# Decoder kernel on one core: second attention taken batch by batch between the expert rows' gathers, and another order in the first attention's slot part

## The chip, the cores and the metric

One core of a Trainium2 chip. The time is device time of one execution, in microseconds (us), median of the runs. Engines: PE is TensorE (matmuls and transposes), DVE VectorE, ACT ScalarE, POOL GpSimd, SP SyncE (which issues most DMAs). Each engine takes its own list of instructions in order, and waits on semaphores that the others raise.

## The reference

Two decoder layers on x of 4 batches, 256 tokens, 256 features (1024 tokens in all), each sublayer followed by residual and layer norm:

```python
x = _layernorm(x + _L0_attn_ref(x, ...))            # slot attention, 16 heads, running sums over tokens
x = _layernorm(x + _L0_xattn_ref(ctx_1024, x, ...)) # state-space scan
x = _layernorm(x + _L0_ffn_ref(x, ...))             # 64 experts, 6 per token, and a shared one
x = _layernorm(x + _L1_attn_ref(x, ...))            # linear attention, 16 heads: the second attention
x = _layernorm(x + _L1_xattn_ref(x, ctx_1024, ...)) # cross attention, 32 heads, rotary positions
x = _layernorm(x + _L1_ffn_ref(x, ...))             # ternary weights
```

The second attention, with heads of 16 features, is

```python
Q = jax.nn.elu(Q) + 1.0
K = jax.nn.elu(K) + 1.0
KV = jnp.einsum('bhsd,bhse->bhde', K, V)
QKV = jnp.einsum('bhsd,bhde->bhse', Q, KV)
out = QKV / (QK_sum[..., None] + 1e-08)
```

followed by the output projection. K and V are summed within one batch, so batches are independent of each other up to and through this sublayer and the projections behind it.

## The kernel before

All work is written out by hand, one list per engine; nothing is planned by a program. Tokens lie in 8 tiles of 128 (`TILES`), two tiles per batch. `xres` holds the residual by token, `xT` its transpose, and `ps` is PSUM with 8 banks.

First attention: a loop over 8 pairs of heads (`step`). In it PE projects values and gates of each tile (`project_vg(t)`, L629, two banks in turn, so tile t waits for the gate of tile t-2, counted from tile 2). ACT copies the values and takes the tanh of the gate (`values_and_gate`), DVE multiplies (`gate(t)`, L1634). Between tiles run the slots: transposes of `okT` (L652), maximum and shift on DVE (L1649, L1651), the exponent `slot_exp` on ACT, its sum and a small product on DVE (L1655, L1659), slot transposes on PE (L661), `wT` on DVE (L1666), then `read(b)` on PE (L594), the mask on DVE (L1621) and `mix(b)` (L681). `read(1)` uses the bank of the gates and waits for gate 7. ACT's order is tiles 0 to 3, slot exponent, tiles 4 and 5, a decay, tiles 6 and 7. PE does tiles 4 to 7 and then the slot transposes. At the same time POOL and DVE run the scan of the second sublayer, whose products POOL makes (L1149, L1156, L1159).

Experts: PE runs groups of four blocks of 128 rows, DVE writes each output (L1931), SP stores it to `y_dram`. When the last is stored, POOL gathers for each token tile its 6 rows, 48 indirect DMAs into a ring of 8 buffers `yg` (L1231). DVE adds each, weighted (L1968); gather n waits for the addition of n-8. After a tile's sixth row DVE takes its statistics (L1615, L1616).

Only when all 48 are added follow, for all four batches at once: layer norm (`norm(2)`, L1776; ACT makes the scale), transposes (`turn_x`, L774) and their copies to `xT` on ACT, query projection (L910), keys and values (L917), the elu in parts on DVE and ACT (L1983 to L2008), key-value products (L928, L930), mask (L2014), read (L941), division (L2018 to L2021), transposes (L951), output projection (L962), residual and statistics (L2030), norm (`norm(3)`), transposes, query projection of the cross attention (L977), rotation (`rotate`, L1901, L1906), the split of the rotated queries into three bf16 parts (casts on ACT, rests on DVE, L2049) and their copies into the stack `q_st` (L1921). The head transposes of the cross attention (L990) then wait for everything stacked, and for POOL's memsets of `q_st`, which wait for `norm(3)` to be complete (L1236). SP's loads of the last layer's weights wait for the same.

## Time and profile before

| | |
|---|---|
| runs | 1192.13, 1201.07, 1199.13 us; median 1199.13 |
| profiled execution | 1193.41 us, its span (first to last instruction) 1191.6 us |
| busy in the span | PE 940.7 us (79%), DVE 809.4 (68%), ACT 499.5 (42%), POOL 374.2 (31%) |
| mean granted clock of TensorE | 0.888 of full |
| chain that ended last | PE 43%, DVE 27%, waiting for nothing shown 8%, DMA 6%, ACT 6%, POOL 6% |

A row of the timeline or of the groups reads: line, engine, operation, output<-inputs, shapes, count, and in brackets the idle time of that engine before it with what ended it. A busy share says how full an engine is and not whether it is late; for that one reads which wait ended last at a place. PE at half clock shows as a granted clock of 0.50 (1.2 GHz against 2.4).

### The profile page before, as it was taken

What the parts mean: (1) busy time and instruction counts of PE and PEld (TensorE: products, weight loads), DVE (VectorE), ACT (ScalarE), POOL (GpSimd) and SP (SyncE); (2) the same over time, 40 slices, a digit from 0 to 9 for tenths busy, and PEclk for the clock granted to TensorE, in tenths of its full rate; (3) what the DMA queues carried; (4) which work ended last, traced back from release to release, by engine and by line L of the source; (5) the groups of instructions that cost most, each with busy time, mean ns of one, the idle gap of its engine ahead of it and who ended that gap; (6) DMA issues with size and microseconds to landing.
All of it is one profiled execution on the core that took longest, in us unless ns stands there. A gap on an engine that the chain in (4) does not pass through costs nothing.

```text
span 1191.6 us, 17024 instructions
## 1 busy us (share of the span) xinstructions
PE 940.7 (79%) x5419; PEld 602.9 (51%) x5423; DVE 809.4 (68%) x1458; ACT 499.5 (42%) x852; POOL 374.2 (31%) x270
## 2 busy tenths in 40 slices
PE   6699998989999899588999899600975776888575
PEld 2366565655656565456666667400573433444333
DVE  6568787777868686968355566344878995555766
ACT  3535344444453444433433345300224444767164
POOL 0035554637273745610433233276010000000000
PEclk9799999999999999779999899855997766989787
DMA  4801121111111111071699999633010000000001
GB/s 156 270 19 66 58 79 53 57 53 57 66 62 49 61 44 45 1 194 38 189 295 297 276 279 290 141 106 97 1 55 17 1 0 1 1 0 1 1 1 36
DMA packets 52585, 104.60 MB, mean 88 GB/s; under 512 B 7513, under 2 KB 25057, under 8 KB 52033
## 3 DMA queue, kind: packets, MB, share of 16 engines
q1 hardware_dynamic: 46785, 88.37, 23.2%
q0 software_dynamic: 5760, 15.74, 5.3%
q8 instruction: 20, 0.33, 0.1%
q14 instruction: 20, 0.16, 0.0%
HBM read 87.14 MB, written 16.94 MB: 87 GB/s over the span
## 4 chain that ended last, share of the span: by engine, by line
PE 43%; DVE 27%; issue 8%; DMA 6%; ACT 6%; POOL 6%; SPq 2%; DVEq 0%; ACTq 0%; POOLq 0%
PE ps L629 6%; PE ps L713 4%; POOL yg L1231 3%; PE ps L594 3%; PE ps L584 3%; PE ps L804 3%; PE ps L990 3%; DVE row_max L2057 3%; PE ps L816 3%; DMA w_dn<-in_w_dn 3%; DMA y_dram<-y_out 2%; PE ps L642 2%; DVE state L1610 2%; PE ps L1033 2%; DVE on L1683 1%
## 5 line engine op out<-in xcount | busy, mean ns | idle before, releaser
L1156 POOL TENSOR_TENSOR state<-state,c_row 128x1024 f32<-128x1024 f32 x32 | 77.3, 2417 | 200.6 <-DVE state L1610 118.0
L629 PE MATMUL ps<-w_vg,xT 128*128 128x512 f32 x256 | 117.8, 604 | 10.2 <-DVE th L1634 10.2
L1204 POOL DMA_INDIRECT xg<-x_dram,tok_of x68 | 65.3, 961 | 154.1 <-PE ps L862 103.9
L1149 POOL TENSOR_TENSOR drive<-du,b_row 128x1024 f32<-128x1024 f32 x32 | 89.4, 2796 | 56.2 <-DVE y L1760 56.2
L804 PE MATMUL ps<-w_gv,xgT 128*128 128x352 f32 (+1 forms) x272 | 91.4, 481 | 1.3 <-DVE y_out L1931 1.3
L1621 DVE TENSOR_TENSOR aT<-ps,tri 128x768 f32<-128x768 f32 x64 | 59.2, 954 | 42.1 <-PE ps L594 42.1
L584 PE MATMUL ps<-xT,w_qks 128*128 128x512 f32 x192 | 85.0, 593 | 0.7 <-DMA w_qks<-in_wqks 0.7
L1610 DVE TENSOR_TENSOR_SCAN state<-decay,drive 128x1024 f32<-128x1024 f32 x32 | 83.5, 2612 | 0.0
L629 PEld LDWEIGHTS ps<-w_vg,xT 128*128 128x128 f32 x256 | 46.6, 192 | 64.7 <-issue 45.5
L2057 DVE TENSOR_REDUCE row_max<-ps 128x1024 f32 x64 | 74.1, 1216 | 7.2 <-PE ps L1005 6.3
L1159 POOL TENSOR_TENSOR y<-y,state 128x1024 f32<-128x1024 f32 x32 | 75.3, 2354 | 2.5
L774 PE MATMUL ps<-ident,xres 128*128 128x128 f32 x64 | 12.9, 365 | 78.3 <-DVE xres L1776 78.3
L1634 DVE SCALAR_TENSOR_TENSOR th<-th,ps 128x256 f32<-128x256 f32 x64 | 26.7, 418 | 66.2 <-ACT th L1260 65.1
L816 PE MATMUL ps<-w_dn,hidT 88*128 88x256 f32 (+1 forms) x272 | 71.2, 384 | 0.0
L1249 POOL COPY v_cols<-x_v 128x64 f32 x32 | 8.6, 270 | 197.7 <-PE ps L1033 181.9
L1931 DVE TENSOR_SCALAR y_out<-ps 128x256 f32<-128x256 f32 x68 | 28.9, 424 | 58.9 <-PE ps L816 31.8
L1260 ACT ACTIVATE probT<-ps 128x1024 f32<-128x1024 f32 x64 | 61.7, 1026 | 14.8 <-PE ps L1019 14.8
L804 PEld LDWEIGHTS ps<-w_gv,xgT 128*128 128x128 f32 x272 | 50.6, 196 | 26.3 <-issue 4.6
L713 PE MATMUL ps<-w_o,oT 128*128 128x256 f32 x256 | 61.8, 391 | 0.0
L1260 ACT ACTIVATE qsT<-ps 128x1024 bf16<-128x1024 bf16 x32 | 32.8, 1024 | 61.8 <-PE ps L990 61.8
L584 PEld LDWEIGHTS ps<-xT,w_qks 128*128 128x128 f32 x192 | 35.4, 190 | 40.2 <-issue 38.5
L1231 POOL DMA_INDIRECT yg<-y_dram,slot_idx x48 | 45.4, 945 | 27.5 <-issue 14.0
(291 smaller groups left out, 2103.9 us busy)
## 6 DMA issues: line engine op xcount, KB each, us to landing
w_gv<-in_w_gv SPq DMA_DIRECT2D x68, 352.0 KB
w_dn<-in_w_dn SPq DMA_DIRECT2D x68, 176.0 KB
y_dram<-y_out SPq DMA_DIRECT2D x68, 128.0 KB, 6.8
b_row<-x_dbl_dram SPq DMA_DIRECT2D x16, 512.0 KB, 3.6
c_row<-x_dbl_dram SPq DMA_DIRECT2D x16, 512.0 KB, 4.7
y_dram<-blank SPq DMA_DIRECT2D x4, 1408.0 KB, 13.0
w_vg<-in_wvg SPq DMA_DIRECT2D x8, 512.0 KB, 3.3
w_qks<-in_wqks SPq DMA_DIRECT2D x8, 384.0 KB, 3.0
```

Source lines behind the costliest of these rows:

```text
L584: last = mm(bank(PJ + n % 2), w_qks[:, k, part * P:(part + 1) * P], xT[:, k, half * 512:(half + 1) * 512], start=(k == 0), stop=(k == KD - 1))
L629: last = mm(bank(PJ + t % 2), xT[:, k, t * P:(t + 1) * P], w_vg[:, k, :], start=(k == 0), stop=(k == KD - 1))
L713: last = mm(ps[:, X + b % 2, 256 * t:256 * t + 256], oT[:, h, c:c + P], w_o[:, h, :], start=(h == 0), stop=(h == 1))
L804: last = mm(ps[:, j, 0:2 * F], x_of(k), w(k), start=(k == 0), stop=(k == KD - 1))
L816: last = mm(ps[:, bk, 256:512], hidT[:, j, f * P:(f + 1) * P], w(f), start=(f == 0), stop=(f == 1))
L1149: G.tensor_tensor(drive[:, n % 2], du[:, e], b_row[:, j], ALU.mult).then_inc(drive_ready, 1)
L1156: G.tensor_tensor(state[:, n % 2], state[:, n % 2], c_row[:, j], ALU.mult).then_inc(read_out, 1)
L1159: G.tensor_tensor(y[:, e], y[:, e], state[:, n % 2], ALU.add).then_inc(y_added, 1)
L1231: G.indirect_dma_start(yg[:, n % 8, :], None, y_dram, bass.IndirectOffsetOnAxis(ap=slot_idx[:, n // TOPK, n % TOPK:n % TOPK + 1], axis=0)) ...
L1260: return nc.scalar.activation(out, in_, func, **kw)
L1610: V.tensor_tensor_scan(state[:, n % 2], decay[:, n % 2], drive[:, n % 2], 0.0, ALU.mult, ALU.add).then_inc(scanned, 1)
L2057: V.tensor_reduce(row_max[:, bass.ds(i * 16 + 4 * b, 4)], pair(4 + 2 * (b % 2)).rearrange("p (a k) -> p a k", a=4), AX.X, ALU.max).then_in ...
```

## The change

Second attention. Each batch is begun when its two tiles are fully added. Five rounds are written out: round r starts batch r (norm, transposes, projections, elu, key-value product, read) and ends batch r-1 (division, output projection, residual, norm, cross attention's query projection, rotation, split and stack). Batches use banks 0 to 3 and 4 to 7 in turn. DVE's list has the additions of gathered rows (`combine`) put between these steps, 12 per round in rounds 0 to 2, after 12 ahead of round 0. Elementwise work takes the two tiles of a batch in one instruction; the buffers `lqT`, `lk`, `lv`, `l_out` shrink to two batches. ACT splits the queries into positive and negative part (four Relu per batch), which DVE did, and makes three of the six stack copies. Keys and queries share `rot`, `part` and `rotated_f32`, and `q_st` and `yg` move in memory (`gap` keeps a stretch free). POOL's and SP's lists are unchanged; their waits for `normed` 32 now mean that the last batch's second norm is done.

First attention. ACT takes tile 4 ahead of the slot exponent, PE does the slot transposes ahead of tile 7, and DVE's `wT` comes ahead of gate 7.

The diff, cut to its core (all it takes away in the second attention is left out; so are `project_out_l`, `attend_l`, `project_x`, `divide_l` and the like, which do for one batch what the old lines did for all):

```diff
+    for r in range(B + 1):
+        for kind, late in kinds:
+            if 0 <= r - late < B:
+                turns[kind, r - late] = len(turns) + 1
+    return turns
...
+NORMED = in_turn(("x2", 0), ("x3", 1))
+SUMMED = {("x2", 0): 1, ("x2", 1): 2, ("x3", 0): 3, ("x2", 2): 4, ("x3", 1): 5, ("x2", 3): 6, ("x3", 2): 7, ("x3", 3): 8}
+MASKED = in_turn(("out", 1), ("kv", 0))
...
+        lqT = sb("lqT", [P, 2, KD, 256])
+        lq_low = sb("lq_low", [P, 2, KD, 256])
+        lk = sb("lk", [P, 2, 2, D])
+        lk_low = sb("lk_low", [P, 2, 2, D])
+        lv = sb("lv", [P, 2, 2, D])
...
+        l_out = sb("l_out", [P, 2, 2, D])
...
-                for t in range(4, TILES):
+                for t in range(4, TILES - 1):
                     project_vg(t)
...
+                project_vg(TILES - 1)
...
+                        c = (2 * b + t) * P
+                        last = mm(ps[:, bank_n, t * 256:(t + 1) * 256], xT[:, k, c:c + P], w[:, k, :], start=(k == 0),
+                                  stop=(k == KD - 1))
+                last.then_inc(done, 1)
+
+            def project_l(b, base):
+                pe.wait_ge(normed, 16 + 2 * NORMED["x2", b])
+                if b >= 2:
+                    pe.wait_ge(attended, b - 1)
+                turn_pair(xres[:, 2 * b:2 * b + 2, :], base)
+                pe.wait_ge(xT_copied, 4 + TURNED["x2", b])
+                for m in range(KD):
+                    for k in range(KD):
+                        last = mm(ps[:, base + 1, m * 256:(m + 1) * 256], l_wq[:, k, m * P:(m + 1) * P],
+                                  xT[:, k, b * 256:(b + 1) * 256], start=(k == 0), stop=(k == KD - 1))
+                last.then_inc(lproj_ready, 1)
+                if b >= 2:
+                    pe.wait_ge(turns_done, 4 * (TILES + b - 1))
+                for t in range(2):
+                    c = (2 * b + t) * P
+                    for k in range(KD):
...
+            for r in range(B + 1):
+                new, old = 4 * (r % 2), 4 * ((r + 1) % 2)
+                if r < B:
+                    project_l(r, new)
+                if r:
+                    project_out_l(r - 1, old)
+                if r < B:
+                    attend_l(r, new)
+                if r:
+                    project_x(r - 1, old)
...
-                for t in range(2, 4):
+                for t in range(2, 5):
                     values_and_gate(t)
                 act.wait_ge(slots_shifted, at(i, 1, 1))
                 f(slot_exp[:], okn[:], ACT.Exp, scale=DK ** -0.5).then_inc(slots_exp, 1)
-                for t in range(4, 6):
-                    values_and_gate(t)
+                values_and_gate(5)
                 decay_of(i, 1)
...
+            def elu_q(b, base):
+                act.wait_ge(lproj_ready, 2 * b + 1)
+                for m in range(KD):
+                    src = ps[:, base + 1, m * 256:(m + 1) * 256]
+                    f(lqT[:, b % 2, m], src, ACT.Relu, bias=l_bq[:, m:m + 1])
+                    last = f(lq_low[:, b % 2, m], src, ACT.Relu, bias=l_nbq[:, m:m + 1], scale=-1.0)
+                last.then_inc(act_step, 1)
+                act.wait_ge(act_step, PAIRS + 2 + b + 1)
+                f(lq_low[:, b % 2], lq_low[:, b % 2], ACT.Exp, scale=-1.0).then_inc(elu_exp, 1)
+
+            def elu_k(b):
+                act.wait_ge(elu_split, b + 1)
+                f(lk_low[:, b % 2], lk_low[:, b % 2], ACT.Exp).then_inc(elu_exp, 1)
...
+            for r in range(B + 1):
+                new, old = 4 * (r % 2), 4 * ((r + 1) % 2)
+                if r < B:
+                    scale_pair("x2", r)
+                    copy_pair("x2", r, new)
+                    elu_q(r, new)
+                if r:
+                    copy_pair("att", r - 1, old + 1)
+                if r < B:
+                    elu_k(r)
+                if r:
+                    scale_pair("x3", r - 1)
+                    copy_pair("x3", r - 1, old + 1)
+                    split_q(r - 1)
...
-                for t in range(6, TILES):
-                    gate(t)
+                gate(6)
                 for n in range(2):
                     c = slice(n * 512, (n + 1) * 512)
                     dve.wait_ge(w_turned, at(i, 2, n + 1))
                     V.tensor_tensor(wT[:, c], bank(Y + n), zT[:, c], ALU.mult).then_inc(wT_copied, 1)
+                gate(7)
...
+            combine_next = iter(range(TILES * TOPK))
+
+            def combine(count):
+
+                for n in itertools.islice(combine_next, count):
+                    t, k = n // TOPK, n % TOPK
                     dve.wait_ge(back[n % 8], 16 * (n // 8 + 1))
                     dve.wait_ge(combined, B + n)
                     V.scalar_tensor_tensor(out=xres[:, t, :], in0=yg[:, n % 8, :], scalar=pick_w[:, t, k:k + 1],
                                            in1=xres[:, t, :], op0=ALU.mult, op1=ALU.add).then_inc(combined, 1)
-                dve.wait_ge(combined, B + TOPK * (t + 1))
-                stats_of(t)
-            norm(2)
-
+                    if k == TOPK - 1:
+                        dve.wait_ge(combined, B + n + 1)
+                        stats_of(t, 2)
...
+            def take_kv(b, base):
+                both = ps[:, base + 2:base + 4, :]
+                dve.wait_ge(lproj_ready, 2 * b + 2)
+                then(V.tensor_tensor(lk[:, b % 2], both[:, :, 0:D], l_bkv[:, 0:D].unsqueeze(1).to_broadcast([P, 2, D]),
+                                     ALU.add))
+                V.tensor_scalar(lk_low[:, b % 2], lk[:, b % 2], 0.0, None, ALU.min).then_inc(elu_split, 1)
+                V.tensor_tensor(lv[:, b % 2], both[:, :, D:2 * D], l_bkv[:, D:2 * D].unsqueeze(1).to_broadcast([P, 2, D]),
+                                ALU.add)
+
...
+            combine(2 * TOPK)
...
+            for r in range(B + 1):
+                new, old = 4 * (r % 2), 4 * ((r + 1) % 2)
+                if r < B:
+                    norm_pair("x2", r)
+                    combine(1)
+                if r:
+                    divide_l(r - 1, old)
+                    combine(1)
+                if r < B:
+                    take_kv(r, new)
+                    combine(2)
+                if r:
+                    add_out_l(r - 1, old)
+                    combine(1)
+                if r < B:
+                    add_bias("x2", r, l_bo)
+                    finish_elu(r)
+                    combine(2)
+                    mask_kv(r, new)
+                    combine(1)
+                if r:
+                    norm_pair("x3", r - 1)
+                    combine(1)
+                    rotate_q(r - 1, old)
+                    combine(1)
+                    add_bias("x3", r - 1, x_bo)
+                    rest_q(r - 1, 0)
+                    combine(1)
+                    rest_q(r - 1, 1)
+                    combine(1)
+                    stack_q(r - 1)
+                else:
+                    combine(6)
```

## Rows read from the trace of the kernel before

**Rows 1.** The page's 40 slices: PE's busy tenths and its granted clock.

```profile
PE   6699998989999899588999899600975776888575
...
PEclk9799999999999999779999899855997766989787
```

**Rows 2.** Windows: busy us (instructions) of PE, PEld, DVE, ACT, POOL; clock, DMA, GB/s.

```profile
770.80:832.90 62.10, 0.00 (x0) 0.00 (x0) 27.52 (x63) 0.00 (x0) 45.38 (x48) 0.50 0.35 102
...
832.90:909.80 76.90, 55.58 (x256) 40.33 (x256) 63.30 (x178) 21.56 (x35) 5.66 (x6) 0.88 0.07 28
```

**Rows 3.** Instructions on the gathered rows: duration ns min/median/max, first and last start.

```profile
L1231 POOL DMA_INDIRECT yg<-y_dram,slot_idx x48: 942/946/955, 770.8 to 829.6; - x48
L1968 DVE SCALAR_TENSOR_TENSOR xres<-yg,pick_w,xres x48: 483/484/486, 773.6 to 832.4; 128x256 f32<-128x256 f32 x48
```

**Rows 4.** Timeline of the first attention, fourth pair, and a start in the fifth.

```profile
237.55 1.06 ACT L1260 ACTIVATE slot_exp<-okn 128x1024 f32<-128x1024 f32 x1 [2.88 <-DVE okn L1651]
...
239.18 0.42 DVE L1634 SCALAR_TENSOR_TENSOR th<-th,ps 128x256 f32<-128x256 f32 x1 [1.67 <-ACT th L1260]
...
239.66 3.70 PE L629 MATMUL ps<-w_vg,xT 128*128 128x512 f32 x8 [1.26 <-DVE th L1634]
...
240.98 0.97 DVE L1659 SCALAR_TENSOR_TENSOR eps_sq<-slot_sum 128x16 f32<-128x16 f32 x1
...
243.20 1.04 PE L661 MATMUL ps<-ident,slot_exp 128*128 128x128 f32 x8
...
245.16 1.58 PE L594 MATMUL ps<-wT,eT 64*128 64x256 f32 x16 [0.93 <-DVE wT L1666]
246.14 0.96 DVE L1621 TENSOR_TENSOR aT<-ps,tri 128x768 f32<-128x768 f32 x1 [0.43 <-PE ps L594]
...
298.71 1.04 PE L661 MATMUL ps<-ident,slot_exp 128*128 128x128 f32 x8
```

**Rows 5.** Groups by shape between 770.8 and 909.8: count, busy us, mean ns.

```profile
L1983 DVE TENSOR_TENSOR lqT<-lqT,lq_low 128x512 f32<-128x512 f32 x4 | 2.7, 685 | 0.1
...
L917 PE MATMUL ps<-l_wkv,xT 128*128 128x512 f32 x32 | 13.9, 592 | 0.0
...
L928 PE MATMUL ps<-lv,lk 128*128 128x128 f32 x32 | 5.4, 293 | 0.0
...
L930 PE MATMUL ps<-ones,lk 128*128 128x8 f32 x32 | 4.1, 236 | 0.0
```

**Rows 6.** Timeline from the last gather to the head transposes.

```profile
834.33 2.67 DVE L1776 TENSOR_SCALAR xres<-xres,ln_rstd,ln_shift 128x256 f32<-128x256 f32 x8
...
835.21 3.40 PE L774 MATMUL ps<-ident,xres 128*128 128x128 f32 x16 [67.51 <-DVE xres L1776]
836.34 0.60 ACT L1260 ACTIVATE xT<-ps 128x512 f32<-128x512 f32 x1 [2.24 <-PE ps L774]
...
888.27 3.51 POOL L1236 MEMSET q_st<- 128x4096 bf16 x1 [57.75 <-DVE xres L1776]
...
890.46 7.17 PE L977 MATMUL ps<-x_wq,xT 128*128 128x256 f32 x32 [0.69 <-ACT xT L1260]
...
892.49 1.42 DVE L1901 TENSOR_TENSOR rot<-ps,cos_sin 128x256 f32<-128x256 f32 x4 [1.61 <-PE ps L977]
893.95 0.76 DVE L1906 TENSOR_TENSOR q_rot<-rot 128x256 f32<-128x256 f32 x2
...
909.82 0.77 PEld L990 LDWEIGHTS ps<-ident_bf,q_st 128*128 128x128 bf16 x8 [12.59 <-DVE q_st L1921]
```

**Rows 7.** Windows of PE alone: PE busy, granted clock, DMA share, GB/s.

```profile
837.00:838.00 1.00, 1.00 (x6) 0.50 0.00 0
...
839.00:840.00 1.00, 0.71 (x2) 1.00 0.00 0
...
479.00:482.00 3.00, 0.00 (x0) 0.64 0.00 0
```

More of the change, by code:

```diff
@@ new lines, in project_out_l, with attend_l @@
+            def project_out_l(b, base):
+                pe.wait_ge(kv_masked, MASKED["out", b])
+                pe.wait_ge(elu_exp, 2 * b + 1)
+                turn_pair(l_out[:, b % 2], base + 1)
+                pe.wait_ge(xT_copied, 4 + TURNED["att", b])
+                project_pair(b, base, l_wo, proj_out_ready)
+            def attend_l(b, base):
+                pe.wait_ge(elu_done, 2 * b + 2)
+                for m in range(KD):
+                    c = slice(m * P, (m + 1) * P)
+                    for t in range(2):
+                        mm(ps[:, base, m * KVW:m * KVW + P], lk[:, b % 2, t, c], lv[:, b % 2, t, c], start=(t == 0),
+                           stop=(t == 1))
+                    for t in range(2):
+                        last = mm(ps[:, base, m * KVW + P:(m + 1) * KVW], lk[:, b % 2, t, c], ones[:, 0:LB],
+                                  start=(t == 0), stop=(t == 1))
+                last.then_inc(kv_ready, 1)
+                pe.wait_ge(kv_masked, MASKED["kv", b])
+                for t in range(2):
+                    for m in range(KD):
+                        last = mm(ps[:, base + 2 + t, m * KVW:(m + 1) * KVW], lqT[:, b % 2, m, t * P:(t + 1) * P],
+                                  kv[:, KD * b + m, :], start=True, stop=True)
+                last.then_inc(kv_ready, 1)
@@ L1461, in cast_key @@
                     act.wait_ge(rotated, 2 * TILES)
-                f(key_part[:, j], key_f32[:], ACT.Copy).then_inc(part_cast, 1)
+                f(part[:, j], rotated_f32[:], ACT.Copy).then_inc(part_cast, 1)
             def stack_key(slot_n):
@@ L1512, in _ @@
-                    f(part[:, j, r], q_rot[:, r], ACT.Copy).then_inc(part_cast, 1)
+                        act.wait_ge(rotated, 2 * (TILES + b + 1))
+                    f(part[:, j, r], rotated_f32[:, r], ACT.Copy).then_inc(part_cast, 1)
+                for slot_n in range(6):
+                    if Q_PARTS[slot_n] == 0:
+                        act.wait_ge(part_cast, 3 + 3 * b + 1)
+                        f(q_st[:, r, :, slot_n * XD_H:(slot_n + 1) * XD_H],
+                          part[:, 0, r].rearrange("p t (h d) -> p t h d", h=XH), ACT.Copy).then_inc(stacked, 1)
@@ L2026, in add_att, with norm_pair @@
-            def add_att(n):
+                    if k == TOPK - 1:
+                        dve.wait_ge(combined, B + n + 1)
+                        stats_of(t, 2)
+            def norm_pair(kind, b):
+                r = slice(2 * b, 2 * b + 2)
+                dve.wait_ge(ln_scale, 4 + 2 * SUMMED[kind, b])
+                then(V.scalar_tensor_tensor(out=ln_shift[:, r], in0=moments[:, r, 0], scalar=-1.0, in1=ln_rstd[:, r],
+                                            op0=ALU.mult, op1=ALU.mult))
+                for t in range(2 * b, 2 * b + 2):
+                    V.tensor_scalar(xres[:, t, :], xres[:, t, :], ln_rstd[:, t:t + 1], ln_shift[:, t:t + 1],
+                                    ALU.mult, ALU.add).then_inc(normed, 1)
@@ new lines, in divide_l @@
+            def divide_l(b, base):
+                r = slice(2 * b, 2 * b + 2)
+                dve.wait_ge(kv_ready, 2 * b + 2)
+                src = ps[:, base + 2:base + 4, 0:KD * KVW].rearrange("p t (k n) -> p t k n", k=KD)
+                then(V.tensor_scalar(l_den[:, r], src[:, :, :, P:KVW], 1e-8, None, ALU.add))
+                then(V.reciprocal(l_den[:, r], l_den[:, r]))
+                for t in range(2):
+                    last = V.tensor_tensor(l_out[:, b % 2, t, :].rearrange("p (k h d) -> p k h d", k=KD, h=LB),
+                                           src[:, t, :, 0:P].rearrange("p k (h d) -> p k h d", h=LB),
+                                           l_den[:, 2 * b + t].unsqueeze(3).to_broadcast([P, KD, LB, P // LB]), ALU.mult)
+                last.then_inc(kv_masked, 1)
```

290 lines of the change are left out of this document (104 added, 186 removed).

## The prediction, made before the changed kernel was run

> **What bounds the kernel now.** I began with the page's line of forty slices and its granted clock, to see which stages keep TensorE (PE) full [rows 1]: the first attention does, and slices 26 and 27 (775 to 834 us) are the emptiest of the run. I then cut that stretch in two with the windows view [rows 2]. From 770.8 to 832.9 PE does nothing: 48 gathers come from GpSimd (POOL) at one in 1.25 us, and VectorE (DVE) adds each [rows 3]. From 832.9 to 909.8 the second attention runs for all four batches at once: 76.9 us, of which DVE is busy 63.3 and PE 55.6. So 139.0 us stand between the first gather and the first head transpose, and DVE works 90.8 of them. The change wants to run the second part under the first. Last, I followed one pair of heads of the first attention in the timeline, because the pairs repeat every 55.5 us (slot transposes at 243.20 and 298.71) and the other edit lies there [rows 4]. Each number below is set against the profiled execution: span 1191.6, its time 1193.4, which is 5.7 below the median 1199.1 of three runs.
>
> **The small edit: slot part of the first attention.** Before, ScalarE (ACT) does the slot exponent (from 237.55, 1.06 us) ahead of tile 4's tanh, so DVE's gate 4 comes at 239.18 and PE's tile 6 begins only at 239.66, after 1.26 us of idling. Then tile 7, then the slot transposes at 243.20, the slot weights on DVE, the read at 245.16 and its mask at 246.14 [rows 4]. With the change tile 4's tanh is ready when DVE has finished the shift, so gate 4 is at about 237.5, and tile 6 follows tile 5 directly at about 238.2. Its two matmuls 512 columns wide take 1.72 (16 such matmuls of the second attention, which the profile lists as 32 records, took 13.9 us [rows 5]), so tile 6 ends at 239.9, the transposes (1.04) at 241.0, tile 7 at 242.7. The small DVE product behind the slot sums (0.97 us for 16 columns) seems to be held until about 241.9, where it ended before [rows 4], and I leave it there; gate 6 and two weight products (0.40, 0.65, 0.65) follow to 243.7, beside tile 7. Tile 7's tanh ends at 243.6 (0.9 behind its matmuls: drain, a copy and the tanh), gate 7 at 244.15, and the mask starts at 244.2 instead of 246.14: 1.95 us less per pair. Behind the mask the order is unchanged and nothing has a time of its own: POOL waits for DVE's scans, and SyncE's weight loads have the same triggers. Eight pairs: **minus 15.6 us**. Bounds: 0, if something behind the mask was due later anyway, and 17, which is 2.1 per pair.
>
> **The large edit, as a list for DVE.** DVE takes its work in order, so I add up its list round by round, with what it waits for. The combines (one gathered row each) cost 0.52 back to back (0.48 and the step to the next), statistics of a tile 0.65, a norm of two tiles 0.94 behind 0.65 of ACT [rows 3, 6]. A pair of tiles in one instruction I price as the 512-wide rows, 0.68 [rows 5]. One batch then holds on DVE: two norms 1.9, two biases 1.2, keys and values 1.7, end of the exponentials 1.2, mask 0.4, division 1.3, residual with statistics 1.9, rotation 2.25 (1.42 and 0.76 with their steps [rows 6]), two rests 1.3, three stack copies 0.6, together 14 us, four batches 56. ACT now takes the split of the queries and three of six stack copies; it is idle most of the stage, so this costs nothing beyond the 1.7 us in the last round below.
>
> What it waits for, PE at full clock: transposes 0.7, copy 0.60 [rows 6], query projection 1.7 (a 256-wide matmul is 0.43: 7.17 us for 16 [rows 6]), keys and values 3.6 with the drain: 6.8 us from the norm to the first key, of which 2.3 are covered by a division and two combines: 4.6 of waiting. Key-value product 2.0 (0.9 for each half batch: 128-wide and 8-wide matmuls side by side, 5.4 and 4.1 us for 32 records [rows 5]), covered to all but 0.4. Transposes, copy and query projection of the cross attention 3.5 from the norm, 2.9 bare. With small ones, 9.2 us of waiting in a full round.
>
> - Before the rounds: 12 combines, gather-bound as now, to 788.5; ACT 0.65.
> - Round 0 (one batch, 12 combines): norm 0.9, chain 6.8, keys and values and two combines 2.7, bias and exponentials 1.9, product and mask 2.5, seven combines and two statistics 4.9, ACT 0.7: 20.4, so to 809.6.
> - Rounds 1 and 2: 12 combines 6.2, statistics 1.3, one batch's work 14.2, waits 9.2: 31.0 each, to 871.5. A gather round alone would be 15.0 [rows 3], so from here POOL waits for DVE: gather n needs combine n-8. Behind a waiting gather POOL's queue holds only further gathers and the memsets of the stack, which the last norm releases, as it does SyncE's two loads of the last layer; that norm is 11 us before the end of the stage and the long memset takes 3.5 [rows 6], so I price it at nothing; without the rotation and the casts beside it, it would be 3.5.
> - Round 3, no combines left: 14 of work and 14 of waits, since nothing fills them: 27.8, to 899.3.
> - Round 4, the last batch alone: division 1.2, PE and copy 3.4, residual 1.9, ACT 0.7, norm 0.9, PE and copy 3.5, rotation 2.3, then casts and rests alternating 3.6, stacks on ACT 1.7: 19.2, to 918.5.
>
> The stage that ended at 909.8 [rows 6] now ends at 918.5: **8.7 us later**, with PE never slow. The overlap gives 44 us (832.9 to 788.5), and the serial chain of each batch, which the old order ran once for all four, takes it back.
>
> **The clock.** The granted clock was 0.50 while PE stood idle and still 0.50 at 837 to 838, nearly 3 us into the transposes; it was 1.00 at 839 [rows 7]. After the first attention PE is idle from 479 to 482 and the mean over these 3 us is 0.64: it fell about 1 us into them [rows 7]. In the old stage, PE is packed, and its clock is 1.00 throughout the projections. In a new round PE has 12.7 us of work at full clock in 31 us, with gaps of 9.7 us between batches (rotation to next norm) and 4.6 before the key-value product. So anything from none to all of this work may double. With all of it at half clock the list above, each PE term doubled, ends at 967.0, or 57.2 more than before. Nearest are the rows on either side of an idle stretch [rows 7], and I go by them: half clock for the first transposes and the query projection (0.4 and 1.7 more), for a quarter of keys and values (0.9), for the key-value product behind its gap (1.8), part of what follows (0.8, some of it hidden): 5.6 per full round, 4.8 in round 0, 6.1 in round 3, 2.9 in round 4, together 25. The stage then ends at 943.4: **plus 33.5 us**.
>
> The Trainium skill speaks against this change here: "TensorE: Matmul & The Clock Gate", section "HAM oscillation — how this bites in real kernels", says that bursts of matmuls with waits between them start cold every time. The trace agrees at the two places named. Taken for all bursts to their end, the rule gives the third rival's time.
>
> **The sum.** 33.5 - 15.6 = +17.9. On the profiled execution 1193.4 that is 1211.3; on the median, 1217. I give 1217.
>
> **The rivals.**
> 1. PE's clock holds (8.7 instead of 33.5): -6.9, 1192. For: the pairs of the first attention, with PE's waits of about a microsecond [rows 4], stand in slices of 0.9 and more [rows 1]. Against: gaps here are longer than the fall took at 479 [rows 7].
> 2. The overlap pays, on the faster side. With round time R the stage ends at 825.6 + 3R. With the small edit's gain the whole is even at R = 33.3, and faster by 1% from R = 29.3 down. The mechanism: DVE's waits in a round (9.2) are mostly filled, because the wide pair instructions cost less than 0.68 and PE answers before its turn, so R is DVE's own work, some 22 to 24: the end is then about 895, 15 less, and with the small edit -30: 1169. Against: the waits follow from the order written out, and no combine stands where the long waits are but one or two.
> 3. Half clock in every burst: +57.2 - 15.6 = +41.6, 1241.
> 4. The small edit does nothing, as something else was due just then (POOL's products, the gate of tile 7 before the second read): +33.5, 1233. For it speaks only that DVE and POOL shut each other out (0.97 us for 16 columns [rows 4]) and could meet anew.
>
> **How the numbers follow.** Forecast 0.50 (1207 to 1227), rival 1 0.17, rival 2 0.10, rival 3 0.12, rival 4 0.11. About 1%, 12 us, is what a measurement of this kernel can tell from no change. Slower by more: four fifths of the forecast, 3 and 4, some 0.62. Within: the rest of the forecast and most of rival 1, 0.27. Faster: 0.11. Eight in ten: from 1188 (rival 1 with the whole small gain) to 1238, which leaves out rival 2 and the top of rival 3.
>
> **What would show it.** Small edit: pairs repeat in 53.6 us instead of 55.5, PE's wait before tile 6 gone, the mask about 2 us nearer to the shift. Large edit: first norm of batch 0 at 18.4 us behind the first gather; rounds of 31 to 37 us; gathers beyond the 20th waiting for DVE's combines; DVE waiting 4.6 to 7.6 for the first keys of each round; head transposes 172 us behind the first gather instead of 139; granted clock of the stage a mixture, 0.5 at each batch's first transposes. I am wrong if a round takes under 29 us, if the clock stays 1.00 across the gaps, or if pairs keep their 55.5.

## The result, and the profile after

The changed kernel took 1211.56 us (median of four runs, 1201.66 to 1215.61) beside 1200.1 for the kernel before: the ratio is 1.0115, with a 95% interval of 1.0072 to 1.0158, so it is 9 to 19 us slower (the two medians by themselves differ by 11.5). The forecast was +17.9. The profiled execution took 1201.66 us, the shortest of the four, with a span of 1199.6 against 1191.6, only 8.0 more. Cut at the same instructions, the two spans give:

| part of the span | before | after | difference |
|---|---|---|---|
| to the last matmul of the first attention (w_o) | 495.6 | 476.3 | -19.3 |
| from there to the experts' first gather list | 71.6 | 69.7 | -1.9 |
| experts, to the first gather of their results | 203.6 | 197.6 | -6.0 |
| first gather to the first head transpose | 139.0 | 174.6 | +35.6 |
| the rest | 281.8 | 281.4 | -0.4 |

The experts are the same code in both. In the profiled runs of the kernels below they took 192.6 to 202.3 us, whichever parts of the change were in, so the 6.0 in the third line is taken as spread from run to run, with the kernel before at the long end of it. The two edits account for about -19 and +36.

The page's slices for the changed kernel:

```profile
PE   6599999999999997678999895365655785888575
...
PEclk9799999999999998898999999667566657999787
```

[Rows 1] had two empty slices, 26 and 27 (counted from 0), and full ones behind them. Now a little work stands in all of slices 25 to 30 and the granted clock is 0.5 to 0.7 in them.

The windows of the stage, cut where each batch's first norm starts (the fifth cut is the division of the last batch), in the columns of [rows 2]:

```profile
743.60:761.96 18.36, 0.00 (x0) 0.00 (x0) 7.03 (x16) 0.50 (x2) 14.09 (x15) 0.51 0.34 100
761.96:787.05 25.09, 13.71 (x44) 10.06 (x44) 11.46 (x27) 3.92 (x9) 13.80 (x16) 0.64 0.26 74
787.05:822.96 35.91, 20.00 (x68) 14.63 (x68) 19.61 (x50) 8.96 (x19) 15.14 (x15) 0.74 0.19 55
822.96:859.79 36.83, 21.05 (x68) 15.48 (x68) 19.41 (x50) 8.96 (x19) 3.97 (x4) 0.64 0.06 18
859.79:894.85 35.06, 21.38 (x68) 15.61 (x68) 13.47 (x34) 7.66 (x16) 0.00 (x0) 0.65 0.00 0
894.85:918.20 23.35, 9.79 (x24) 6.47 (x24) 8.93 (x25) 6.05 (x12) 4.65 (x6) 0.57 0.23 90
```

Read the first figure (the length) against DVE's, the third. In no round is DVE busy for much more than half of it, and PE, at two thirds of its speed, is not full either. What is long is neither engine's work but their turns.

The gathers and the combines, to compare with [rows 3] (the last two lines: what GpSimd sat idle for ahead of a gather, and DVE's combines):

```profile
L1252 POOL DMA_INDIRECT yg<-y_dram,slot_idx x48: 941/947/1150, 743.6 to 836.7; - x48
...
  DVE xres L2024: 29.5, 11
```

```profile
L2024 DVE SCALAR_TENSOR_TENSOR xres<-yg,pick_w,xres x48: 464/480/486, 746.3 to 857.0; 128x256 f32<-128x256 f32 x48
```

The last gather starts 93.1 us behind the first instead of 58.8: GpSimd now waits for combines, eleven times. That hurts nobody: DVE's 13.3 us of waits for gathers all lie ahead of the first norm, none in the rounds.

One full round, the second (engine, line and tile as in [rows 6]):

```profile
787.05 0.19 DVE L2033 SCALAR_TENSOR_TENSOR ln_shift<-moments,ln_rstd 128x2 f32<-128x2 f32 x1 [0.60 <-ACT ln_rstd L1281]
...
788.16 1.12 PE L918 MATMUL ps<-ident,xres 128*128 128x128 f32 x4 [4.54 <-DVE xres L2036]
...
789.96 3.78 PE L938 MATMUL ps<-xT,l_wq 128*128 128x256 f32 x8 [0.69 <-issue]
...
793.54 4.35 PE L946 MATMUL ps<-l_wkv,xT 128*128 128x512 f32 x8
...
797.92 0.69 DVE L2047 TENSOR_TENSOR lk<-ps,l_bkv 128x512 f32<-128x512 f32 x1 [7.76 <-PE ps L946]
...
801.04 0.69 DVE L2081 TENSOR_TENSOR xres<-xres,ps 128x512 f32<-128x512 f32 x1 [0.39 <-PE ps L926]
...
805.17 1.15 PE L961 MATMUL ps<-lv,lk 128*128 128x128 f32 x4 [4.17 <-DVE lk L2057]
...
808.72 0.44 DVE L2062 TENSOR_TENSOR kv<-ps,head_mask 128x272 f32<-128x272 f32 x1 [2.15 <-PE ps L964]
...
814.96 1.42 DVE L1954 TENSOR_TENSOR rot<-ps,cos_sin 128x256 f32<-128x256 f32 x4 [4.17 <-PE ps L926]
...
822.96 0.16 DVE L2033 SCALAR_TENSOR_TENSOR ln_shift<-moments,ln_rstd 128x2 f32<-128x2 f32 x1 [0.95 <-ACT ln_rstd L1281]
```

Follow the chain: shift, transposes, a copy, queries, keys and values, and 10.9 us on DVE can take the keys, having sat idle for 7.76 of them. The query projection takes 3.78 us here. The three longest waits of DVE for PE in it are 14.1 us in sum. TensorE's clock in the same round, in windows of PE alone:

```profile
794.00:795.00 1.00, 1.00 (x2) 0.50 0.13 49
795.00:796.00 1.00, 1.00 (x3) 0.98 0.00 0
...
806.00:812.00 6.00, 5.47 (x26) 0.50 0.20 57
```

It was 0.50 from the transposes at 788.16 on, through the query projection, and came up at 795, in the middle of keys and values, where the old stage had it up by 839, right behind its transposes [rows 7]. After the gap of 4.17 us ahead of the key-value product it is 0.50 again, from 806 to 812. The groups of the stage by shape show the sum of it, to compare with [rows 5]:

```profile
L2055 DVE TENSOR_TENSOR lqT<-lqT,lq_low 128x512 f32<-128x512 f32 x4 | 2.7, 684 | 0.0
...
L946 PE MATMUL ps<-l_wkv,xT 128*128 128x512 f32 x32 | 15.4, 627 | 0.0
...
L961 PE MATMUL ps<-lv,lk 128*128 128x128 f32 x32 | 9.6, 456 | 17.8 <-DVE lk L2057 17.8
...
L964 PE MATMUL ps<-ones,lk 128*128 128x8 f32 x32 | 6.9, 326 | 0.0
```

DVE's 512-wide instruction costs 0.68 us in both. The key-value matmuls take 456 and 326 ns instead of 293 and 236: these suffer most, since they stand behind the gap; keys and values, in the middle of a burst, only 627 instead of 592.

Last, one pair of the first attention, the fourth, and the slot transposes of the fifth, to compare with [rows 4]:

```profile
226.62 5.32 PE L643 MATMUL ps<-w_vg,xT 128*128 128x512 f32 x12
...
229.25 0.41 DVE L1686 SCALAR_TENSOR_TENSOR th<-th,ps 128x256 f32<-128x256 f32 x1
...
229.37 1.06 ACT L1281 ACTIVATE slot_exp<-okn 128x1024 f32<-128x1024 f32 x1 [0.17 <-DVE okn L1703]
...
231.77 1.04 PE L675 MATMUL ps<-ident,slot_exp 128*128 128x128 f32 x8
...
231.92 1.85 DVE L1711 SCALAR_TENSOR_TENSOR eps_sq<-slot_sum 128x16 f32<-128x16 f32 x1
...
234.76 1.89 PE L608 MATMUL ps<-wT,eT 64*128 64x256 f32 x16 [0.24 <-DVE wT L1717]
...
235.25 0.42 DVE L1686 SCALAR_TENSOR_TENSOR th<-th,ps 128x256 f32<-128x256 f32 x1
...
235.73 1.92 DVE L1673 TENSOR_TENSOR aT<-ps,tri 128x768 f32<-128x768 f32 x2
...
285.06 1.04 PE L675 MATMUL ps<-ident,slot_exp 128*128 128x128 f32 x8
```

Tiles 4, 5 and 6 are now one run of matmuls (5.32 us, no wait in it), gate 4 comes ahead of the slot exponent, and the mask starts 6.36 us behind that exponent instead of 8.59.

### The profile page after: what moved, and what is told of

Its sections match the earlier page's. It is cut to its first block, busy times and chain, and to the rows that moved or that the text cites. A ratio compares the mean times of both kernels' runs of the same rounds, so it can differ in the third digit from the quotient of the medians.

```text
span 1199.6 us, 17036 instructions
## 1 busy us (share of the span) xinstructions
PE 960.7 (80%) x5439; PEld 620.6 (52%) x5439; DVE 805.0 (67%) x1418; ACT 513.5 (43%) x894; POOL 376.4 (31%) x270
## 4 chain that ended last, share of the span: by engine, by line
PE 52%; DVE 28%; issue 9%; ACT 8%; POOL 2%; DMA 1%; DVEq 0%; SPq 0%; ACTq 0%; POOLq 0%
PE ps L831 5%; PE ps L819 5%; PE ps L643 4%; PE ps L728 4%; PE ps L608 3%; PE ps L1011 3%; PE ps L598 3%; DVE row_max L2150 2%; PE ps L926 2%; DVE state L1662 2%; PE ps L656 2%; PE ps L1026 2%; PE ps L877 1%; PE ps L825 1%; ACT probT L1281 1%
## 5 line engine op out<-in xcount | busy, mean ns | idle before, releaser
L1225 POOL DMA_INDIRECT xg<-x_dram,tok_of x68 | 66.6, 980 | 149.5 <-PE ps L877 93.9
L643 PEld LDWEIGHTS ps<-w_vg,xT 128*128 128x128 f32 x256 | 46.2, 191 | 47.3 <-issue 44.2
L1281 ACT ACTIVATE probT<-ps 128x1024 f32<-128x1024 f32 x64 | 61.6, 1026 | 13.3 <-PE ps L1040 13.3
L1252 POOL DMA_INDIRECT yg<-y_dram,slot_idx x48 | 47.0, 980 | 57.5 <-DVE xres L2024 29.5
L1281 ACT ACTIVATE v<-ps 128x256 f32<-128x256 f32 x64 | 24.4, 381 | 69.5 <-PE ps L643 69.2
L728 PEld LDWEIGHTS ps<-w_o,oT 128*128 128x128 f32 x256 | 47.8, 194 | 11.3 <-issue 5.9
```

The lines of the kernel that those rows point to most:

```text
L643: last = mm(bank(PJ + t % 2), xT[:, k, t * P:(t + 1) * P], w_vg[:, k, :], start=(k == 0), stop=(k == KD - 1))
L728: last = mm(ps[:, X + b % 2, 256 * t:256 * t + 256], oT[:, h, c:c + P], w_o[:, h, :], start=(h == 0), stop=(h == 1))
L1225: G.indirect_dma_start(xg[:, j, :], None, x_dram, bass.IndirectOffsetOnAxis(ap=col, axis=0)).then_inc(gathered[j], 16)
L1281: return nc.scalar.activation(out, in_, func, **kw)
```

## Experiments

The theory after the result: the small edit gives 2.2 us in each pair; the batches in rounds cost a chain of turns between DVE, PE and ACT that is run through four times, at half clock for much of it, and the overlap with the gathers is worth less than that. The rivals: the loss comes from the combines that were put into the chain; from the half clock alone; or from GpSimd, whose gathers now wait. Each time is set against the kernel before on the same chip.

### The two edits by themselves

e1_small_only has the change of the first attention alone:

```diff
                 for t in range(2):
                     values_and_gate(t)
-                for t in range(2, 4):
+                for t in range(2, 5):
                     values_and_gate(t)
 ...
-                for t in range(4, TILES):
+                for t in range(4, TILES - 1):
                     project_vg(t)
 ...
+                project_vg(TILES - 1)
```

> The kernel before with the small edit alone (ACT's tile 4 ahead of the slot exponent, PE's slot transposes ahead of tile 7, DVE's weights ahead of gate 7). My theory: the gain is local to the slot part and repeats in each of the eight pairs: slot transposes 53.4 us apart instead of 55.6, the loop 16 to 19 us shorter, the stage from first gather to head transposes unchanged at 139, the whole 1180 to 1185 in median, so some 1.5% under the kernel before. Rival: the 6 us that the expert part was shorter in the changed kernel's trace belong to this edit too (another clock or another meeting of the weight transfers): then the whole is 22 to 27 us faster, 1174 to 1178. Rival: the gain of the loop is given back in the expert part, which is bound by transfers: then the whole gains under 8 us.

Measured: 1168.59 against 1187.33, ratio 0.984 (0.9815 to 0.9867), 18.7 us less. Pairs repeat every 53.37 us instead of 55.63 (one seventh of the time from the first slot transpose of the first pair to the last one of the eighth; that is 0.1 more than from start to start, 55.51 in [rows 4], in every kernel, and drops out of the differences); the stage of the second attention is 139.2 long. e10_small_again is the same kernel once more, beside the kernel of the last experiment:

> The small edit alone once more, on the same chip as the one with the fillers: 1.5 to 1.7% under the kernel before (0.984 in its first run), a stage of 139 us from the first gather to the head transposes.

It gave 1169.56 against 1189.87, ratio 0.9833 (0.9804 to 0.9861), stage 139.2.

e2_large_only leaves the first attention as it was and has all the rest of the change.

> The changed kernel with the small edit undone. My theory: the large edit alone costs what the stage lost, 35.6 us from first gather to head transposes (174.6 against 139.0), and nothing elsewhere: 1230 to 1237 in median, pairs at 55.6 us again. Rival: the large edit also gained something in front of the stage, as the 6 us in the expert part (buffers lie elsewhere in memory, shared tiles): then the first gather comes near 765 instead of 771 and the whole is 1224 to 1229.

Measured: 1222.25 against 1187.33, ratio 1.0288 (1.0261 to 1.0315), 34.9 us more; stage 175.1; pairs 55.63. So the edits add: -18.7 and +34.9 make +16.2, inside the interval of the whole change. The stage by itself, small edit alone, then large edit alone (windows, columns as above):

```profile
746.50:885.70 139.20, 55.80 (x257) 39.99 (x257) 90.81 (x240) 21.57 (x35) 51.03 (x54) 0.71 0.20 61
```

```profile
765.70:940.80 175.10, 87.31 (x272) 62.83 (x272) 79.95 (x200) 36.03 (x76) 51.57 (x54) 0.64 0.16 48
```

DVE works 10.9 us less in the new stage (wide pair instructions, and ACT took over the split of the queries and three of the six stack copies: 36.03 us instead of 21.57), and the stage is 35.9 longer. PE's busy time rises by 31.5 for the same products: the groups above show them longer, line by line, at the lower clock. Neither could be read from the engine totals of the kernel before.

### The small edit in halves

e5_small_act changes only ACT's order (tile 4's tanh ahead of the slot exponent); e6_small_pe only the place of tile 7's projection on PE, and gate 7 on DVE.

> The kernel before with only ScalarE's half of the small edit: tile 4's tanh ahead of the slot exponent; TensorE's order and the gates' order on VectorE as before. Theory (the gain is the wait of 1.26 us before tile 6 and nothing else of this half): the pair shortens by 1.1 to 1.3 us, since tiles 6 and 7 and all that hangs on them come that much sooner; eight pairs give 9 to 10 us, period 54.4 instead of 55.6. Rival (the slot exponent, now 0.6 us later, holds up the slot sums and with them the small product of VectorE beside GpSimd's step, so that this half alone gains little and TensorE's half brings nearly all): period 55.2 or more, gain under 4 us.

> The kernel before with only the other half of the small edit: on TensorE the slot transposes ahead of tile 7, on VectorE gate 7 behind the slot weights; ScalarE's order as before. Theory: TensorE still waits 1.2 us before tile 6, and what is gained is that tile 7 (1.7 us) runs beside VectorE's slot weights: 1.0 to 1.2 us per pair, period about 54.5, gain 8 to 10 us, so that the two halves add up to the 2.25 us per pair of both. Rival (each half needs the other, because tile 7 moved alone only moves the wait): period 55.2 or more, gain under 4 us, and the whole edit more than the sum of its halves.

Measured, beside 1189.7: e5 1182.91, ratio 0.9947 (0.9916 to 0.9978), pairs 54.49; e6 1184.07, ratio 0.9949 (0.9925 to 0.9973), pairs 54.80. Per pair that is 1.14 and 0.83, together 1.97, and both at once give 2.25. ACT's half is what was expected. The other half gives less alone, because gate 7 now stands ahead of the masks while tile 7's tanh still comes late. In e6 DVE sits idle for 0.97 us before that gate, and the second read waits for it:

```profile
242.38 0.42 DVE L1635 SCALAR_TENSOR_TENSOR th<-th,ps 128x256 f32<-128x256 f32 x1 [0.97 <-ACT th L1261]
...
242.85 0.92 PE L594 MATMUL ps<-wT,eT 64*128 64x256 f32 x8 [0.35 <-DVE th L1635]
```

With ACT's half as well, gate 7 is done at 235.67 and PE's reads run on without a stop (1.89 us for the 16 records). The expectation for e5 held in its period (54.4); that for e6 did not: 1.0 to 1.2 us per pair were expected and 0.83 came, and its whole gain, 5.6 us, is under the 8 to 10 given. The whole gain of e5, 6.3 us by the ratio, is also under its 9 to 10, though the interval (2.6 to 10.0) reaches them. And the halves do not simply add: their sum is 0.28 us per pair short of both together.

### No overlap at all

e7_combines_first keeps the rounds, but has all 48 combines ahead of the first:

```diff
-            combine(2 * TOPK)
+            combine(TILES * TOPK)
```

Beside this, the counts at which ACT takes up each batch's statistics follow the new order (`MOMENTS`), since the statistics of all gathered tiles are now taken ahead of the first norm.

> The changed kernel, but all 48 combines ahead of the first norm: the batches still follow one another in the rounds of the change, and nothing of the second attention runs beside the gathers. Theory (a round of 35 to 37 us is TensorE's and VectorE's chain, and most of a round's twelve combines, 7.5 us with the statistics, lies in waits or would otherwise be replaced by waiting): the gathers take 62 as before, the rounds shorten only to about 30, the stage from the first gather to the head transposes lasts 62 + 22 + 3 x 30 + 23, about 195 to 200 instead of 174.6, and the time is some 22 us over the changed kernel's. Rival (the combines are what made the rounds long, the chains fit into little over 23 us without them): the stage stays within 180, and the time within 6 us of the changed kernel's.

Measured: 1239.62 against 1189.7, ratio 1.043 (1.039 to 1.0471); stage 207.9. Its windows, up to the first norm and from there:

```profile
748.90:811.50 62.60, 0.00 (x0) 0.00 (x0) 27.95 (x64) 0.50 (x2) 45.38 (x48) 0.50 0.35 101
811.50:956.80 145.30, 82.99 (x272) 60.13 (x272) 54.41 (x137) 35.42 (x74) 4.65 (x6) 0.69 0.04 15
```

This falls beyond both expectations: 195 to 200 and rounds of about 30 in mine, under 180 in the rival's. The first norm is 44.2 us later than in the changed kernel (62.6 against 18.4), as counted; but its rounds, 18.1, 34.7, 36.2, 33.3 and 23.0, stand against 25.1, 35.9, 36.8, 35.1 and 23.4 with the combines in them. In round 0 they cost 7.0 us: there seven of the twelve stand in one row between the mask and the next norm. In rounds 1 and 2 the same twelve, 7.5 us of DVE with their statistics, cost 1.2 and 0.6. They lie in the waits. (Round 3 has no combines in either kernel and still differs by 1.8, at a clock of 0.76 against 0.65, so a difference of this size says only that the cost is small.) So the overlap works and gives 33.3 us. What it is set against is the chain: 145.3 us from the first norm to the heads for what the old order did in 76.9 [rows 2].

### The waits filled

e3_combines_in_waits moves the twelve combines of a round to three places, 6 ahead of the keys, 2 ahead of the mask, 4 ahead of the rotation:

```diff
                 if r < B:
                     norm_pair("x2", r)
-                    combine(1)
 ...
                 if r < B:
+                    combine(6)
                     take_kv(r, new)
-                    combine(2)
```

> The changed kernel; only DVE's additions of gathered rows are placed elsewhere: 6 ahead of the keys, 2 ahead of the mask, 4 ahead of the rotation, where DVE stands waiting for PE 7.8, 2.2 and 4.2 us a round. My theory: a round is a chain of PE, ACT and DVE steps, and additions cost only where they stand in the chain (10 of 12, 0.5 us each, and the statistics): rounds 1 and 2 fall from 36 to 30 or 31 us, round 0 by 3, the stage from 174.6 to about 161, the whole by 12 to 14 us. Rival: DVE's own amount of work or the gathers' supply sets the round: moving them changes nothing, within 3 us. Rival: the gathers now come too late, since eight buffers are freed in lumps of six: rounds 0 to 2 grow by the wait, some 3 us each, and the whole gains under 4.

Measured: 1199.19 against 1187.33, ratio 1.0106 (1.0077 to 1.0135); stage 167.8, 6.8 shorter, half of what was expected. The waits of DVE in the stage, changed kernel first (us in total, times, longest):

```profile
DVE lk L2047 <- PE ps L946: 32.2, 4, 9.4
DVE rot L1954 <- PE ps L926: 22.6, 4, 6.8
...
DVE kv L2062 <- PE ps L964: 10.7, 4, 3.7
DVE xres L2081 <- PE ps L926: 7.8, 4, 5.7
```

```profile
DVE lk L2047 <- PE ps L946: 21.3, 4, 8.6
DVE rot L1954 <- PE ps L926: 16.5, 4, 5.5
...
DVE kv L2062 <- PE ps L964: 10.5, 4, 3.2
DVE xres L2081 <- PE ps L926: 9.8, 4, 5.7
```

The two long waits lost 17.0 us, but the rounds are 21.7, 34.7, 36.4, 33.3 and 23.2: half of the gain is in round 0, where e7 had shown combines on the path; rounds 1 and 2 gave 1.2 and 0.4, as much as leaving the combines out altogether. Round 3 has none in either kernel, and its 1.8 us came with a clock of 0.76 instead of 0.65. DVE's waits are where it meets the chain; in rounds 1 and 2 the chain was already running beside most of the combines, and putting the rest of them into waits shortened next to nothing.

### The clock held up

e4_warm_fill lets PE do matmuls of no use (128x512, their result is overwritten) in its gaps, with nothing else changed; e8_warm_and_waits has these and the combines of e3.

```diff
+            def fill(count, bank_n):
+                for _ in range(count):
+                    mm(bank(bank_n), ident[:], l_wkv[:, 0, :], start=True, stop=True)
 ...
+                    fill(4, new)
                     attend_l(r, new)
 ...
                     project_x(r - 1, old)
+                if r < B:
+                    fill((4, 7, 7, 6)[r], old)
```

> The changed kernel with idle matmuls on PE in the gaps of the second attention's rounds (3 before round 0, 4 before each key-value product, 4 to 7 behind each cross attention projection, 3 in the last round; 0.86 us each at full clock), which write banks that the next step overwrites; the output is unchanged. My theory: about 25 us of the 35.6 lost in the stage are half clock: with the gaps filled the granted clock of the stage is near 1.00, each wait for the first keys is 4.6 us instead of 7 to 8, rounds 1 to 3 fall from 36 to 31 us, and the stage from 174.6 to 152 to 160. Rival: the clock hardly matters, since the waits are semaphores' and other engines' time: the stage stays within 3 us of 174.6 or grows by the fillers. Rival: the fillers overshoot their gaps at half clock (1.7 us each) and lengthen the chain: the stage grows to 180 or more.

> The changed kernel with both remedies at once: the filler matmuls that kept the clock up, and the combines placed in groups of 6, 2 and 4 ahead of the instructions that wait longest. Theory (alone the moved combines gave 6.8 us of the stage, because TensorE at half clock set the round; with TensorE at full clock they should give what was first counted for them): rounds 1 and 2 fall from 32 to 27 or 28, the stage to 143 to 149 us instead of 157.5 and 174.6, and the time is some 10 us under that of the filler matmuls alone. Rival (the round is bound by the serial chain through TensorE whatever its clock): the stage stays at 153 or more.

Measured: e4 1183.75 against 1187.33, ratio 0.9981 (0.9959 to 1.0002), stage 157.5. e8 1176.43 against 1189.7, ratio 0.9896 (0.9857 to 0.9936), stage 149.5. The stage in e4, then in e8:

```profile
739.30:896.80 157.50, 111.05 (x364) 66.18 (x364) 79.83 (x200) 36.04 (x76) 51.64 (x54) 0.85 0.18 54
```

```profile
743.50:893.00 149.50, 107.83 (x365) 63.27 (x366) 81.99 (x200) 36.03 (x76) 51.36 (x54) 0.87 0.19 57
```

PE does 25 us more and the stage is 17.1 shorter; the clock is 0.85 instead of 0.64. The stage lies in the range expected for e4, the way there only in part: the first keys were to be waited for 4.6 us a round, and the four waits are still 29.4 us instead of 32.2. What shrank is DVE's wait for the key-value product (10.7 to 4.3), for the rotation (22.6 to 16.9) and for the residual (7.8 to 5.6). The four kernels make a square:

| stage, us | combines spread | combines in three groups |
|---|---|---|
| clock as it falls | 174.6 | 167.8 |
| clock held up | 157.5 | 149.5 |

The clock is worth 17.1 and 18.3, the placing 6.8 and 8.0, and in the sum each hardly depends on the other. After e3 my explanation was that PE at half clock hid the rest of the 13 us counted for the placing; then it should have come out in the lower row. 8.0 came, and the stage of e8 is half a microsecond over the range given (against the kernel before it is 10 us better than e4, as expected). So that explanation does not carry the 13 us. Round by round it is not quite dead: e4's rounds are 23.6, 32.7, 31.9, 32.0 and 18.9, those of e8 20.4, 29.2, 30.8, 29.5 and 21.2. In rounds 1 and 2 the placing gives 4.6 us with the clock held up, where it gave 1.6 without; but rounds 3 and 4, in which no combine was moved, differ by 2.5 and -2.3 as well, so how much of the 4.6 is the placing stays open. What e7 and e3 show together holds for the clock as it falls: most of the combines were not on the chain in the first place. With both remedies the stage is still 10 us longer than the old one, at 87% of full clock, and its rounds 1 to 3 take 29 to 31 us each at a granted clock of 0.94 to 1.00: the half clock alone is not the loss.

### Warm ahead of the old order

e9_small_warm is the small edit alone, with fillers at the two places where the old second attention meets an idle PE.

> The small edit alone, with the old second attention, and filler matmuls on TensorE in two idle stretches: eight of 512 columns from the 44th combine on, ahead of the second norm, and 22 of 256 columns ahead of the head transposes. Theory (the clock has to be up when the serial stretch begins): the sixteen transposes behind the norm take about 1.9 us instead of 3.6, the first head transposes 0.8 instead of 1.03, the stage from the first gather to the head transposes 137 instead of 139.2, and the time is 2 to 3 us under that of the small edit alone. Rival (the clock rises a little later than the fillers start, or the transposes wait for VectorE anyway): no difference beyond 1 us.

Measured: 1167.49 against 1189.87, ratio 0.9815 (0.9788 to 0.9842), beside 0.9833 for e10 on the same chip: no difference that can be told. The fillers and the transposes behind them, small edit alone first:

```profile
810.86 3.64 PE L775 MATMUL ps<-ident,xres 128*128 128x128 f32 x16 [67.48 <-DVE xres L1776]
```

```profile
806.55 8.65 PE L908 MATMUL ps<-l_wkv,ident 128*128 128x512 f32 x16 [60.43 <-DVE xres L1978]
815.03 1.91 PE L775 MATMUL ps<-ident,xres 128*128 128x128 f32 x16
```

The transposes took 1.91 us as expected, and they began 65.8 us behind the first gather instead of 64.4, since the fillers ran past the norm. The stage is 139.0 beside 139.2. The fillers ahead of the head transposes gave nothing either: the first eight records took 1.03 us in both kernels, where 0.8 was expected. Fewer fillers ahead of the norm might have kept the gain; that was not tried.

The best version without fillers is the small edit alone, at 0.984: 1.6% under the kernel before and some 2.7% under the changed one.

## Why the prediction was right

The sign and the balance held: a gain in the first attention, a larger loss in the second, and both for the reasons given. +17.9 was forecast; +13.8 by the ratio, with 9 to 19 in the interval, was measured. That the sum came so near is luck in part: the first attention gained 2.3 us more than forecast (8 x 2.24 against 15.6) and the stage lost 2.1 more, and the two nearly cancel. The parts as measured add up to +17.7 (35.6 less 17.9); the 4 us between that and the ratio lie within the interval and are not explained. In the range, the lower bound of 1188 does not follow from the terms named for it: 1199.1 + 8.7 - 17 is 1191.

- **Small edit.** Forecast 1.95 per pair; 2.24 measured (53.39 instead of 55.63, counted as above). The steps are in the timeline in the order in which I listed them. The term that was too large is the last: I had gate 7 end 6.6 us behind the start of the slot exponent and the mask at 6.65; it ended at 6.3 and the mask began at 6.36, since gate 6 and the weight products took 0.2 less than counted and tile 7's tanh was there 0.2 earlier. Up to the last w_o matmul the kernels with this edit end 17.2 to 19.3 us sooner, where 15.6 was forecast; my upper bound of 17 was too low.
- **DVE's small product.** Held to the same point as before, as I left it: it takes 1.85 us where it took 0.97, and ends at the end of GpSimd's product (233.74 against 233.77).
- **DVE's list and its waits.** In the second round 14.8 us of waiting were counted (9.2, and 5.6 for the half clock). The three waits for PE, one for the residual and one for the shift add up to 15.4: 7.76, 2.15, 4.17, 0.39 and 0.95.
- **The rounds.** Forecast 25.2, 36.5, 36.5, 33.9 and 22; measured 25.1, 35.9, 36.8, 35.1 and 23.4. The stage was forecast at 172.5 and took 174.6. The first norm came 18.4 us behind the first gather, as forecast.
- **The clock.** I put 24.8 us on it, between 0 and 57. The fillers won back 17.1 with a granted clock of 0.85; what the rest of the way to 1.00 is worth was not measured. The 25 are therefore consistent with the runs, not shown by them: in e4, rounds 1 and 2 take 32.7 and 31.9 us at 0.90 and 0.95, near the 31.0 listed for full clock, but rounds 0 and 3 take 23.6 and 32.0, at 0.86 and 0.84, where 20.4 and 27.8 were listed. A part of what I booked as clock may be the list's own. My places of half clock were right for the transposes, the queries and the key-value product and somewhat low in the last two rounds, which is the 2.1 us by which the stage is longer.
- **The idle stretch at 479.** I wrote that PE is idle from 479 to 482 after the first attention and that the clock fell 1 us into it. The stretch lies ahead of the last output projections, and PE had stood idle since 476.9: its granted clock was still 1.00 from 477 to 479, 0.91 in the next microsecond and 0.50 from 480 on. So the fall came 3 us behind the last matmul and not 1. The argument against rival 1 stands even so, since the gaps are longer than that too: those of 4.54, 9.02 and 9.02 us ahead of rounds 1 to 3 and that of 4.17 us within round 1 were each followed by 0.50.
- **What I had right for a wrong reason.** I priced the twelve combines of a round at 7.5 us on the path and the waits on top of them. The sum came out, but e7 shows that a full round without combines is only about 1 us shorter. Combines and waits stand in for each other there: in e7 DVE is busy 6.0 and 5.8 us less in rounds 1 and 2, and idle 4.8 and 5.1 us more. For the forecast it made no difference. For e3 it did, where I expected 13 us from moving combines into waits and got 6.8.
- **Rival 1** (the clock holds) is excluded by 0.50 in the rounds, **rival 2** by rounds of 35 and more, **rival 3** by 795 to 800 at full clock, **rival 4** by e1. In the Trainium skill, "TensorE: Matmul & The Clock Gate", section "HAM oscillation — how this bites in real kernels", has bursts begin cold when the wait ahead of them was long. The rounds agree: each one's first transposes ran at 0.50. In rounds 0 to 3 the clock came back later in the same burst; in the last it stayed at 0.50 from 896 to 911.
- **Stalls moved.** GpSimd waits 29.5 us for combines, and in the rounds themselves DVE waits for no gather: of the stage's 13.3 us of such waits all lie ahead of the first norm. So it costs nothing, as priced.

## What to carry to other kernels

Splitting a stage into batches to start it earlier repeats its serial chain for each batch: add up that chain (here some 35 us from one norm to the next, with two batches in flight) before counting what overlaps, and ask what the stage was bound by in one piece. A wait on an engine is a hole that work can be put into, but it shortens nothing unless that work stood on the chain; whether it did is told by a run without the work, not by the list of the engine, and only for the clock at which that run was made. A stage cut into short bursts also loses TensorE's clock, which was worth 17 us here and could be bought back with matmuls of no use, if they end before the real ones are due.

## What the runs showed of the hardware

- TensorE's granted clock was at 0.50 (1.2 GHz) again after the gaps of 4.54 and 4.17 us in the second round, and came back at 795 (0.98 in the next microsecond, then 1.00), behind transposes from 788.16 and the query projection. In the kernel before it was 0.50 up to 838 and 1.00 at 839 [rows 7], with nothing but transposes since 835.21 [rows 6] and the first projection starting at 839.29. The rise doesn't come at a fixed place in the order of the work.
- A small instruction of DVE with two operands in SBUF was held until GpSimd's product ended: 128x16 elements took 0.97 us (before), 1.82 (e5) or 1.85 (after) according to when it met it, each time to within 0.03 us of the product's end, and 0.17 us in the first pair, where no product was running. The Trainium skill, "Trainium Architecture — The Big Picture", section "What this means for kernel authors", calls the pair's port an exclusive lock; these rows agree.
- Gathers and combines hardly disturb one another here. In the changed kernel a combine took 0.48 us beside gathers (746 to 761) and 0.48 behind the last of them (854 to 857). A gather's median was 947 ns, and 946 in the kernel before; its longest was 1150 instead of 955, and the long ones start while DVE is at work (1.14 us at 800.34, with two combines from 799.59).
